# Query projection in three fp32r terms behind the third key block, and chunk 1's first key and value products ahead of chunk 0's first scores

## What is computed

```
q = layernorm(x) @ Wq.T * 32**-0.5          # 16 heads of 32
k, v = ctx @ Wk.T, ctx @ Wv.T
x = x + (sigmoid(q k^T) v, heads joined) @ Wo.T
x = x + a causal linear attention of layernorm(x)
x = x + a gated MLP of layernorm(x), 512 -> 2048 -> 2048 -> 2048 -> 512
```

## Time and profile before

| | us |
|---|---|
| median of 3 runs | 1899.4 |
| lowest and highest | 1898.33, 1899.59 |
| the profiled execution, its own time | 1899.09 |
| its span in the profile | 1897.1 |
| PE busy in the span | 1887.3 |
| DVE busy | 1211.3 |
| ACT busy | 1021.1 |

### The profile page before, as it was taken

One profiled execution on the slowest core, in us unless ns is written; L12 is line 12 of the kernel. 1 busy time (PEld: TensorE's weight loads), 2 busy tenths in 40 slices (PEclk: granted clock), 3 DMA queues, 4 the chain that ended last, 5 costly groups with the idle time before them and its releaser, 6 DMA issues.

```text
span 1897.1 us, 51012 instructions
## 1 busy us (share of the span) xinstructions
PE 1887.3 (99%) x19436; PEld 1710.1 (90%) x19436; DVE 1211.3 (64%) x2139; ACT 1021.1 (54%) x1157; POOL 4.8 (0%) x18
## 2 busy tenths in 40 slices
PE   9999999999999999999999999999999999999999
PEld 8899999998898999999989899999998989878998
DVE  7676666667667666666766766766676675566322
ACT  6455455554545545555454554555545445556864
POOL 0000000000000000000000000000000000000000
PEclk9999999999999999999999999999999999999999
DMA  7556455655555655555555565555655555455784
GB/s 228 153 151 176 130 157 156 158 159 153 157 149 156 171 131 157 156 156 160 153 155 149 158 171 132 155 159 154 161 151 153 150 160 140 119 155 222 281 297 165
DMA packets 130875, 310.92 MB, mean 164 GB/s; under 512 B 33936, under 2 KB 37008, under 8 KB 112272
## 3 DMA queue, kind: packets, MB, share of 16 engines
q1 hardware_dynamic: 96160, 207.28, 41.3%
q10 hardware_dynamic: 34672, 103.04, 17.3%
HBM read 153.95 MB, written 0.52 MB: 81 GB/s over the span
## 4 chain that ended last, share of the span: by engine, by line
PE 98%; DMA 1%; DVE 0%; ACT 0%; ACTq 0%; issue 0%; SPq 0%
PE kp L891 25%; PE vp L916 24%; PE sc L932 20%; PE acc L952 18%; PE ps L1803 6%; PE ps L1788 1%; PE py L1816 1%; PE qk_p L1481 1%; PE vp L1000 0%; PE sc L1017 0%; DMA weights<-wv_dram 0%; DMA probs<-wkT_dram 0%; PE kp L980 0%; PE qk_p L1550 0%; PE acc L1178 0%; PE ps L1766 0%
## 5 line engine op out<-in xcount | busy, mean ns | idle before, releaser
L429 ACT ACTIVATE probs<-sc 128x1024 f32<-128x1024 f32 x784 | 770.2, 1026 | 737.8 <-PE sc L932 583.4
L891 PE MATMUL kp<-x_combos,weights_r 128*128 128x256 f32 x4032 | 521.7, 278 | 0.0
L916 PE MATMUL vp<-more_weights,x_combos 128*128 128x256 f32 x4032 | 513.8, 277 | 2.3 <-DVE v L701 2.3
L891 PEld LDWEIGHTS kp<-x_combos,weights_r 128*128 128x128 f32 x4032 | 486.6, 188 | 9.8 <-issue 9.5
L916 PEld LDWEIGHTS vp<-more_weights,x_combos 128*128 128x128 f32 x4032 | 483.7, 188 | 3.1 <-DVE v L701 2.5
L932 PE MATMUL sc<-rows_r,k_stack_r 96*128 96x256 f32 x3136 | 437.1, 281 | 0.1
L932 PEld LDWEIGHTS sc<-rows_r,k_stack_r 96*128 96x128 f32 x3136 | 393.8, 189 | 21.7 <-issue 20.6
L952 PE MATMUL acc<-probs,v 128*32 128x256 f32 x6272 | 354.4, 380 | 0.0
L676 DVE TENSOR_TENSOR parts<-parts,kp 128x512 f32<-128x512 f32 x240 | 164.5, 685 | 278.1 <-PE kp L891 278.1
L952 PEld LDWEIGHTS acc<-probs,v 128*32 128x32 f32 x6272 | 195.9, 110 | 131.4
L613 DVE TENSOR_TENSOR x_combos<-ctx_raw,x_combos 128x512 fp32r<-128x512 f32 x240 | 166.1, 692 | 8.2
(11 more groups left out here) (217 smaller groups left out, 890.1 us busy)
## 6 DMA issues: line engine op xcount, KB each, us to landing
k_stack_r<-k_rows_hi SPq DMA_DIRECT2D x784, 64.0 KB, 2.3
k_stack_r<-k_stack_r SPq DMA_DIRECT2D x196, 256.0 KB, 3.0
k_stack_r<-k_rows_lo SPq DMA_DIRECT2D x780, 64.0 KB, 2.6
ctx_raw<-ctxT_dram ACTq DMA_DIRECT2D x48, 1024.0 KB, 6.3
weights<-w_all_dram ACTq DMA_DIRECT2D x176, 256.0 KB, 3.7
w_raw<-w_all_dram SPq DMA_DIRECT2D x44, 1024.0 KB, 4.8
weights<-wqk_dram ACTq DMA_DIRECT2D x2, 1024.0 KB, 9.4
probs<-wvT_dram SPq DMA_DIRECT2D x2, 512.0 KB, 7.6
```

The lines of the kernel that those rows point to most:

```text
L429: nc.scalar.activation(probs[:, place(par, n), :], sc[g % 2][:], ACT.Sigmoid).then_inc(probs_ready, 1)
L891: last = nc.tensor.matmul(k2[:, r, :], wk[i - 1][:, k, a, r * P:(r + 1) * P], xc[:, i - 1, k, b, :], start=i in FRESH and r == 0 and n == ...
L916: last = nc.tensor.matmul(v2[:, r, :], xc[:, i - 1, k, b, r * P:(r + 1) * P], wv_c[i - 1][:, k, a, :], start=i in FRESH and r == 0 and n == 0,
```

## The change

Three things are edited.

The projection: the copies of the transposed x become fp32r hi (ACT, into `xnT[0]`) and get lo parts (two 128x512 subtractions on DVE); the query weights get a hi part (one 128x2048 activation on ACT, behind `v0_part(1)`) and a lo part (one 128x2048 subtraction on DVE, between the second and the third sum of key weights). The parts of the weights lie in the tensor into which the queries are stacked later. PE multiplies the three terms (x hi, w hi), (x hi, w lo), (x lo, w hi), 16 matmuls each.

The order: on PE `k_block(2)` moves ahead of the projection, the rest is then `v_block(2)`, `k_block(3)`, `v_block(3)`. On ACT `v0_part(0)` moves ahead of `x0_round(4)` and `k0_part(1)`, and `k0_part(2)` ahead of the queries' hi part; on DVE `k0_rest(2)` moves ahead of their lo part.

Chunk 0: `alone()` starts with `keys(1)` and `values(1)`, only then waits for the stacked queries and takes `pair(0)`; each later pair up to `pair(3)` stands behind its products instead of ahead of them. On ACT, `k_part` and `v_part` come ahead of the first sigmoid, behind a wait for the stacked queries, and `k_first` and `v_first` behind the second sigmoid. SP waits for the fourth score unit before it stacks chunk 1's keys.

```diff
-        xnT = spare[:, 2048:3072].rearrange("p (k l) -> p k l", k=KE)
+        spare_r = kst[:, 1, :, :, :, :].rearrange("p i j r n -> p (i j r n)")
+        xnT = [spare_r[:, 2048 + 1024 * b:3072 + 1024 * b].rearrange("p (k l) -> p k l", k=KE) for b in range(2)]
+        wq = [qst[:, 2 * b:2 * b + 2, :, :].rearrange("p j g l -> p (j g l)").rearrange("p (k n) -> p k n", k=KE)
+              for b in range(2)]
...
                 if k_next and split_next:
+                    if first:
+                        sp.wait_ge(scores_ready, 4)
                     for q in range(4):
                         stack_rows(m, q, True)
...
             x0_round(3)
+            v0_part(0)
             x0_round(4)
             k0_part(1)
-            v0_part(0)
             for a in range(LT):
                 queries_from(a)
...
             v0_part(1)
+            act.wait_ge(wq_loaded, 16)
+            nc.scalar.activation(wq[0], wq_raw, ACT.Copy).then_inc(qx_hi, 1)
             for n in range(5, 9):
                 wk_round(n)
             for n in range(5, 9):
                 wv_round(n)
+            k0_part(2)
             act.wait_ge(q_made, 1)
             nc.scalar.activation(qr_hi, sc[0][:], ACT.Copy, scale=SCALE).then_inc(q_hi, 1)
             to = f32(qst[:, :, :, :])
-            k0_part(2)
             act.wait_ge(q_lo, 1)
...
-                saved = (0, 3) if par == 0 and not first else (1, 3)
+                saved = (0, 3) if par == 0 else (1, 3)
+                if first:
+                    act.wait_ge(q_moved, MOVED)
+                    act.wait_ge(q_stacked, 2 * MOVED)
+                    k_part(m)
+                    v_part(m)
                 for n, at in enumerate(BY_HALF):
                     sigmoid(c, par, n, at, first)
-                    if k_next and n == saved[0]:
+                    if first and n == 1:
+                        k_first(m)
+                        v_first(m, 1 - par)
+                    elif first and n == 3:
+                        act.wait_ge(x_ready, c * 7 + 7)
+                        nc.scalar.dma_start(raw[:], ctxT[c + 2]).then_inc(ctx_loaded, 16)
+                    elif first:
+                        pass
+                    elif k_next and n == saved[0]:
...
             k0_rest(1)
-            for n in range(1, 5):
+            for a in range(LT):
+                dve.wait_ge(qx_hi, a + 1)
+                at = slice(a * P, (a + 1) * P)
+                nc.vector.tensor_tensor(xnT[1][:, :, at], rows_of(a), f32(xnT[0][:, :, at]),
+                                        ALU.subtract).then_inc(qx_rest, 1)
+            for n in range(1, 3):
+                w_sum(wk_raw, wk_sum, n, wk_summed)
+            dve.wait_ge(qx_hi, LT + 1)
+            nc.vector.tensor_tensor(wq[1], wq_raw, f32(wq[0]), ALU.subtract).then_inc(qx_rest, 1)
+            for n in range(3, 5):
                 w_sum(wk_raw, wk_sum, n, wk_summed)
...
             wv_rest(6)
+            k0_rest(2)
             dve.wait_ge(q_hi, 1)
...
-            k0_rest(2)
             wv_rest(7)
...
             v_block(1)
-            pe.wait_ge(wq_loaded, 16)
-            pe.wait_ge(xnT_ready, LT)
+            k_block(2)
+            pe.wait_ge(qx_hi, LT + 1)
             pe.wait_ge(k_lo, 1)
-            for g in range(G):
-                for k in range(KE):
-                    last = nc.tensor.matmul(sc[0][:, g * L:(g + 1) * L], wq_raw[:, k, g * P:(g + 1) * P],
-                                            xnT[:, k, :], start=k == 0, stop=k == KE - 1)
+            for n, (x, w) in enumerate(X_FIRST):
+                if w:
+                    pe.wait_ge(qx_rest, LT + 1)
+                elif x:
+                    pe.wait_ge(qx_rest, LT)
+                for g in range(G):
+                    for k in range(KE):
+                        last = nc.tensor.matmul(sc[0][:, g * L:(g + 1) * L], wq[w][:, k, g * P:(g + 1) * P],
+                                                xnT[x][:, k, :], start=n + k == 0 and g % 2 == 0,
+                                                stop=n == 2 and k == KE - 1, skip_group_check=True)
             last.then_inc(q_made, 1)
-            for q in range(2, 4):
-                k_block(q)
-                v_block(q)
+            v_block(2)
+            k_block(3)
+            v_block(3)
             for ready in (wk_ready, wv_ready):
                 pe.wait_ge(ready, 8)
-            pe.wait_ge(q_moved, MOVED)
-            pe.wait_ge(q_stacked, 2 * MOVED)
...
                 def alone():
-                    pair(0)
                     keys(1)
                     values(1)
-                    pair(1)
+                    pe.wait_ge(q_moved, MOVED)
+                    pe.wait_ge(q_stacked, 2 * MOVED)
+                    pair(0)
                     keys(2)
                     values(2)
-                    pair(2)
+                    pair(1)
                     keys(3)
                     values(3)
-                    pair(3)
+                    pair(2)
                     keys(4)
                     values(4)
+                    pair(3)
                     weigh(c, par, range(8), order, first)
```

More of the change, by code:

```diff
@@ L201, in cross_attention @@
         var_ready, sd_ready, xn_ready = sem("var_ready"), sem("sd_ready"), sem("xn_ready")
-        xnT_made, xnT_ready, q_made = sem("xnT_made"), sem("xnT_ready"), sem("q_made")
+        xnT_made, qx_hi, qx_rest, q_made = sem("xnT_made"), sem("qx_hi"), sem("qx_rest"), sem("q_made")
         one_ready, zeros_ready, rows_zero = sem("one_ready"), sem("zeros_ready"), sem("rows_zero")
@@ L280, in cross_attention, with rows_of @@
         HALVES = (slice(0, HE), slice(HE, E))
+        def rows_of(a):
+            return sc[1][:, a * E:(a + 1) * E].rearrange("p (k l) -> p k l", k=KE)
         def transposed_norm(a, h):
@@ L416, in queries_from @@
                 act.wait_ge(xnT_made, a + 1)
-                nc.scalar.activation(xnT[:, :, a * P:(a + 1) * P], sc[1][:, a * E:(a + 1) * E].rearrange(
-                    "p (k l) -> p k l", k=KE), ACT.Copy).then_inc(xnT_ready, 1)
+                nc.scalar.activation(xnT[0][:, :, a * P:(a + 1) * P], rows_of(a), ACT.Copy).then_inc(qx_hi, 1)
             def sigmoid(c, par, n, at, first):
```

## The result

| kernel | median, us | lowest, us | executions |
|---|---|---|---|
| before, on the same chip | 1898.99 | 1897.24 | 22 |
| changed | 1901.68 | 1899.15 | 22 |

The ratio is 1.0018, with a 95% interval of 1.0009 to 1.0026: the change costs 1.7 to 4.9 us, 2.7 by the medians, 0.14% of the time. The prediction was 1901.7. The profiled execution has a span of 1900.3 us, 3.2 more than before.

A forecast was written before the change was run, and what follows sets the result against it. PE was taken to bound the kernel, busy 1887.3 of 1897.1 us. `v_block(3)` 2.26 us late and chunk 0 costing 0 gave 1899.09 + 2.3 = 1901.4, or 1901.7 against the median; range 1899.0 to 1904.4.

The forecast's parts named there:

- a granted clock below 1 between 30 and 45 us: Sign around chunk 0's start: if the granted clock showed below 1 there, the forecast was wrong.
- Start of `v_block(3)`: On PE ahead of chunk 0: starts at 36.55 instead of 34.29, 2.26 us late, waiting for `v0_part(2)`.
- The chain: DVE sums, ACT roundings, queries' hi and lo parts, DMA issues: each pushed back, key-weight sum 4.3 us, hi part 4.8 us.
- the issues hold ACT: On ACT: four DMA issues take 2.79 us, so `v0_part(2)` comes only at 35.9; said to decide 2.8 us.
- The two gaps: New PE waits: 1.5 us ahead of `k_block(3)` for `k0_rest(2)`, 2.1 us ahead of `v_block(3)`.
- The projection gained: Query projection on PE: 48 fp32r matmuls take 5.66 us instead of 6.72, a gain of 1.06.
- the rival in which slower terms are hidden too: PE's projection: fp32r terms no faster than 0.14 each, ending at 28.5, hidden by ACT's chain; forecast stands, no chance given.
- The check from PE's side, 2.5: PE up to chunk 0: 0.25 and 1.06 won, 0.25, 1.5 and 2.1 lost, 2.5 us net.
- the wait for the queries: Chunk 0: stacked queries land at 40.8, `pair(0)` wants them at 42.1, so the new order covers the wait.
- the order of chunk 0 costs nothing: Chunk 0 on PE: same number of instructions, only their order changes, 0 us.
- Chunk 2's context: DVE casts its first piece at 56.6; `keys(6)` may start at 62.0, PE reaches it at 62.5, so 0 us.
- the fall of the clock: Rival: the gap ahead of `v_block(3)` lowers PE's clock, adding 1.5 to 1.8 us, to 1903.4; chance 0.17.

The follow-up runs named there:

- the one with zeros: The changed kernel with eight matmuls of zeros on PE between `k_block(3)` and `v_block(3)`; median 1899.66 us, ratio 1.0009 to the kernel before.
- in due order: The changed kernel with ACT's and DVE's queues put in the order in which work falls due; median 1897.28 us, again 1897.81 us.

## Why the prediction was right

The mechanism held: what the preparation pushed back on DVE and ACT decided, and each step of that chain came within about 0.2 us. The hit of 1901.7 on 1901.68 is in part luck. The forecast was 2.3 over a median of 1899.4; with 22 executions the kernel before stands at 1898.99 and the changed one 2.7 above it, so two errors of 0.4 cancelled. And the 2.7 is not made of what the 2.3 was made of: only some 1.1 us show in executions without a fall of the clock. By one of its own signs, a granted clock below 1 between 30 and 45 us, the forecast was wrong in the first profile. The steps are compared with both profiles, the mark with the second, which had no fall.

- *Start of `v_block(3)`*: predicted 36.55, measured 36.46 and 36.32. Its delay, measured from `v_block(0)`, is 2.05 and 2.03 where 2.26 was predicted; at the mark it is 2.23 where 2.3 was. The 0.2 between them is pace: behind its wait `v_block(3)` takes 2.93 instead of 2.83, and the first two products 0.1 more together.
- *The chain*: third sum of key weights 23.55, measured 23.44; queries' hi part 30.85, measured 30.72; lo part 31.9, measured 31.77; the issues hold ACT until 35.9, measured 35.75. That the issues hold ACT was the step that decided 2.8 us, argued from one row of the loop; it held.
- *The two gaps*: predicted 1.5 and 2.1, measured 1.14 and 1.76. The matmuls between them ran slower than the 0.118 us that I took for all of them: from 23.58 to 27.45 the last 32 take 0.121 each, and the blocks behind a wait take 2.9. The projection gained 0.7 rather than 1.06, and with its wait 0.5 rather than 0.8 (from 21.25 to 27.45 is 6.2, with 0.17 of waiting, against 6.72). `v_block(1)`, on the other hand, starts at 15.47, 0.24 sooner than predicted. Since ACT's chain set the end, neither moved it, and the rival in which slower terms are hidden too describes this. The check from PE's side, 2.5, was 0.2 over the sum already in the prediction, and its terms were less good than the chain's.
- *Chunk 0*: the wait for the queries was covered, and `keys(3)` in the second profile follows its pair at 46.65 with no wait, where I had put the margin at 0.1. That the order of chunk 0 costs nothing did not hold for the kernel that has it alone: 0.5 us there. Chunk 2's context, forecast at 56.6, was cast at 54.20 in the second profile and at 56.83 in the first, behind the fall; `keys(6)`, at 64.11 in the first, did not wait in either.
- *What I gave too little*: the fall of the clock, to which I gave 0.17. It came in the first of the two profiles of the changed kernel, and cost 1.55 (predicted 1.5 to 1.8). By the mean clocks 13 of the changed kernel's 34 executions are at 0.998 or less, and 8 of 97 of the kernel before: falls come in some executions and not in others, and more often in the changed kernel.

The Trainium skill counts four passes for true FP32 (FP8 and Floating Point Precision, TensorE Precision Notes); the estimate from it, three passes and 5.04 us, does not fit the rows, which give the projection 6.0 us without its wait. The Trainium skill's 50 ns for a sequencer's dispatch (DMA: Bandwidth & Descriptors, Anatomy of one DMA) is for GpSimd's path, and an issue on ACT takes 0.68 us here.

## What to carry to other kernels

A faster operation that needs prepared operands moves work to the engines that prepare them. Where these work their lists in order, cost what the preparation pushes back, down to the last thing that the bounding engine waits for, and only then count what it saves. A DMA issue counts as an instruction of the engine that makes it, here 0.65 to 0.90 us on ACT: put what others wait for ahead of it, not behind. Of two waits in a row on one engine, the earlier may be worth nothing. And where kernels differ by a few us, look at the mean granted clock of each execution before reading a difference of medians as work.

## What the runs showed of the hardware

**A gap of PE lowers its clock in some executions and not in others.** Behind the same waits (1.14 and 1.76 us) the granted clock fell in one profile of the changed kernel and not in the other. Nor did it fall in the kernel with the old order of chunk 0, which has the same two waits. Behind 3.39 and 3.55 us it fell in both kernels that had them. The gap of 1.9 to 2.6 us near the end of the cross attention, which all kernels have the earlier trace rows, is followed by a fall in ten of the thirteen profiles, and by none in the changed kernel's second, in the one with zeros and in the first in due order, where the gap is 2.36, 2.06 and 1.96 us. Once a fall followed shorter gaps: with `k0_part(2)` earlier the clock was at 0.50 from 1738 to 1744 us, behind gaps of 0.68 and 0.67 us, near 1724 and 1734, that every profile has ahead of the MLP.

**A fall costs one of two amounts here.** Near the end of the cross attention it cost 1.3 to 1.5 us (5.3 to 5.5 from the product's start to the `acc` matmuls, 4.0 to 4.1 without), and 1.5 in chunk 0 of the changed kernel and of the one with `k0_part(2)` earlier. Twice it lasted longer: 3.1 us in chunk 0 of the kernel in due order with the old order of chunk 0 (6.79 instead of 3.65, the clock at 0.50 from 40 to 46 us), and 3.2 in the MLP with `k0_part(2)` earlier (224.0 us from those `acc` matmuls to the end, 220.7 to 221.2 in the profiles with the usual pace).

**The last stage has two paces.** Of the thirteen profiles, two show the MLP's 128x256 matmuls at 281 ns instead of 276 with the granted clock at 1.00 in both (in a third, the one of the fall above, one group is slower for the clock). The groups of the MLP from 1740 to 1850 us, first in the changed kernel's second profile, then in the one with `v0_part(2)` ahead (busy us, mean ns | idle before):

```profile
L1841 PE MATMUL ps<-weights_r,w_hi 128*128 128x256 f32 x512 | 58.2, 276 | 0.0
```

```profile
L1841 PE MATMUL ps<-weights_r,w_hi 128*128 128x256 f32 x512 | 60.5, 281 | 0.0
```

From the first matmul of the MLP to the end it is 171.55 us against 165.93, 5.6 us, which is why that kernel's span is 1904.4 us though its mark is at +1.77. The kernel in due order shows the one pace in its first profile and the other in its second, so no edit alone sets it. What does stays open.

**The time of a DMA issue varies.** The four issues of the queries' lo part, the same instructions each time, took ACT 2.73 us in the changed kernel, 3.60 with the float32 projection, and 3.15 and 2.59 in the two profiles of the one kernel in due order.
